# A recurrent layer's step: state's products copied and scanned in halves, two banks of negated sums put into PSUM by ScalarE

## The reference, cut to what matters

```python
def _L0_cond_ref(x, h0, Wx, Wh, b):          # x (16, 128, 128), h0 (16, 128)
    xw = jnp.einsum('ntd,dh->nth', x, Wx) + b
    def step(prev_h, xw_t):
        next_h = jnp.tanh(prev_h @ Wh + xw_t)
        return (next_h, next_h)
    _, hs = jax.lax.scan(step, h0, jnp.swapaxes(xw, 0, 1))
    return jnp.swapaxes(hs, 0, 1)
```

## Time and profile before

| | us |
|---|---|
| median of 3 runs | 8404.59 (8403.8 to 8407.73) |
| the profiled execution, whole | 8408.27 |
| its span, first to last instruction | 8406.4 |
| the recurrent loop's 127 intervals between new states | 320.5 to 5085.3 |
| a usual step | 37.12 |
| the step at a turn of the loop (7 of them) | 42.3 to 43.1 |

### The profile page before, as it was taken

How to read it: one execution, slowest core, us unless ns; L and a number is a source line. 1 busy time by engine, 2 the same in 40 slices (tenths; PEclk the granted TensorE clock), 3 DMA queues, 4 the chain that set the end, 5 groups by cost and what they waited for, 6 DMA issues and landing times. The chain is left out here.

```text
span 8406.4 us, 121771 instructions
## 1 busy us (share of the span) xinstructions
PE 7003.6 (83%) x39089; PEld 2814.9 (33%) x39089; DVE 7019.4 (84%) x12568; ACT 4731.0 (56%) x5718; POOL 1750.4 (21%) x1386
## 2 busy tenths in 40 slices
PE   4799999899998999999999994488888888782889
PEld 1333333333333333333333331122222222341453
DVE  4799999999999999999999996899999999446333
ACT  3677777777777777777777773233333333222322
POOL 0000001011010000101101000377777777000000
PEclk8999999999999999999999997799999999896999
DMA  1111111111111111111111111000000000000000
GB/s 38 35 27 31 29 29 32 27 31 27 32 31 27 31 30 29 32 26 32 28 30 32 26 32 29 18 4 3 4 3 4 3 4 3 2 6 3 3 15 5
DMA packets 51335, 174.64 MB, mean 21 GB/s; under 512 B 5857, under 2 KB 13794, under 8 KB 49698
## 3 DMA queue, kind: packets, MB, share of 16 engines
q0 software_dynamic: 37264, 145.91, 9.8%
q1 hardware_dynamic: 13586, 22.47, 1.0%
HBM read 15.12 MB, written 7.34 MB: 3 GB/s over the span
## 5 line engine op out<-in xcount | busy, mean ns | idle before, releaser
L944 POOL TENSOR_TENSOR hc<-hh,cg 128x512 f32<-128x512 f32 x1024 | 1294.8, 1267 | 512.1 <-DVE hh L927 512.1
L320 PE MATMUL r_ps<-wdiag,whq 128*128 128x512 bf16 x4864 | 1165.4, 382 | 233.1 <-ACT rx_d L389 174.4
L872 ACT ACTIVATE ps_m<-ps_m,aneg 128x508 f32<-128x508 f32 x1024 | 673.2, 658 | 1192.9 <-DVE hh L927 1071.5
L927 DVE TENSOR_TENSOR_SCAN hh<-ps_m,bx 128x512 f32<-128x512 f32 x1024 | 1257.2, 1235 | 0.0
L459 POOL TENSOR_TENSOR r_gate<-ident 128x1 f32<-128x1 f32 x137 | 213.7, 1560 | 4561.3 <-DVE rx_s L547 4496.2
L843 PE MATMUL ps_m<-hc,pick 128*128 128x512 f32 x2048 | 1053.4, 598 | 2.1 <-POOL hc L944 0.8
L554 DVE TENSOR_TENSOR_SCAN co<-rh_d 128x772 f32<-128x772 f32 x512 | 862.6, 1748 | 207.5 <-ACT rh_d L389 207.5
L554 DVE TENSOR_TENSOR_SCAN co<-rx_d 128x772 f32<-128x772 f32 x544 | 924.1, 1762 | 0.0
L909 DVE TENSOR_TENSOR bx<-ps_m,bg 128x512 f32<-128x512 f32 x1024 | 699.2, 689 | 49.3 <-PE ps_m L856 49.2
L320 PEld LDWEIGHTS r_ps<-wdiag,whq 128*128 128x128 bf16 x4864 | 417.8, 98 | 934.7 <-DVE rh_gain L183 219.8
L854 PE MATMUL ps_m<-rows,ones 128*128 128x512 bf16 x1024 | 405.3, 396 | 268.7 <-ACT ps_m L872 264.4
(11 more groups left out here) (407 smaller groups left out, 11796.8 us busy)
## 6 DMA issues: line engine op xcount, KB each, us to landing
rx_nd<-rx_s POOLq DMA_DIRECT2D x137, 1040.0 KB, 8.0
rows_scratch<-pc SPq DMA_DIRECT2D x48, 128.0 KB
rows<-rows_scratch SPq DMA_DIRECT2D x128, 48.0 KB
ew<-in_e SPq DMA_DIRECT2D x3, 1024.0 KB, 7.7
co<-in_x_dn SPq DMA_DIRECT2D x1, 1024.0 KB, 4.8
xcur<-in_x_dn SPq DMA_DIRECT2D x1, 1024.0 KB
out_x<-xcur SPq DMA_DIRECT2D x1, 1024.0 KB, 3.9
qi<-in_f_q SPq DMA_DIRECT2D x1, 384.0 KB, 3.0
```

Source lines behind the costliest of these rows:

```text
L320: e.matmul(ps[:, bank, :], whq[:, 0, :], wdiag[:, 0, 0:N, :].rearrange("p m k -> p (m k)"), start=True, stop=True)
L872: e.activation(da[un % NDA][:, :, 1:T], ps[:, un % 2, :].rearrange("p (n t) -> p n t", n=NG4)[:, :, 1:T], ACT.Exp, scale=aneg[:, 0:1]).the ...
L927: e.tensor_tensor_scan(hh[un % NBUF][:], da[un % NDA].rearrange("p n t -> p (n t)"), bx[un % NBUF][:], 0.0, ALU.mult, ALU.add).then_inc(sc ...
L944: e.tensor_tensor(hc[un % NHC][:], hh[un % NBUF][:], cg[:], ALU.mult).then_inc(weighted, 1)
```

## The change

The state's side of `rnn()` is changed in five places, and the X side in one.

- ACT copies R's products in two instructions in place of four, one for each half of the sequences (all four banks, 1024 elements). `rp_mm` is told once, after the last matmul of all banks.
- DVE's odd scan is split by halves of the sequences, for R and for X. R's two halves each wait for their copy. X's first half stays ahead of R's scans, X's second half comes after R's differences, ahead of X's even sums. `xs` counts three a step.
- PE forms negated sums by matmul for banks 4 and 5 alone. For banks 6 and 7 ACT writes the negated sums into PSUM, and PE waits for that ahead of the differences' matmul on bank 6.
- ACT's `put_sums` for R is split into odd and even places. ACT's order after the copies: odd sums, `Sign`, the write into PSUM, `Tanh`, even sums, differences.
- PE has 2 fillers in place of 5 between `residue` and R's remainder.

```diff
-        KA = NB + 4 + 2 * NRC + 1
-        VSUM = 3 + NRC + 1
+        A_COPIED, A_ODD, A_SEEDED, A_SIGNED, A_PUT = 2, 3, 5, 6, 8
+        KA = A_PUT + 2 * NRC + 1
+        V_ODD, V_EVEN, V_DIFF = 2, 3, 4
+        VSUM = V_DIFF + NRC + 1
...
+        OWN = NB // 2
+        HALVES = (slice(0, N // 2), slice(N // 2, N))
...
 # PE, h_product
                     for b in range(NB):
                         ins = e.matmul(ps[:, bank0 + b, :], h_stat(b, q), h_mov(b, r), start=(i == 0), stop=(i == 5))
-                        if i == 5:
-                            ins.then_inc(rp_mm, 1)
+                ins.then_inc(rp_mm, 1)
 # PE, remainder(..., own=NB, seeded=None)
                 e.wait_ge(*prefixed)
-                for b in range(NB):
+                for b in range(own):
                     e.matmul(ps[:, bank0 + b, :], negid[:], piece(F, "s", b), start=True, stop=False)
                 e.wait_ge(*differenced)
                 for b in range(NB):
+                    if b == own:
+                        e.wait_ge(*seeded)
+                    e.matmul(ps[:, bank0 + b, :], ident[:], diff(b), start=False, stop=False, skip_group_check=(b >= own))
-                    e.matmul(ps[:, bank0 + b, :], ident[:], diff(b), start=False, stop=False)
 # PE, a step
-                    residue(0, (ra, KA * t + NB)).then_inc(rl_mm, 1)
-                    stay_warm(4, 5)
-                    remainder(4, R, h_stat, h_mov, (v, KV * t + V0 + 2), (v, KV * t + V0 + 3), h_diff, False)
-                    sticky(4, (ra, KA * t + NB + 2))
+                    residue(0, (ra, KA * t + A_COPIED)).then_inc(rl_mm, 1)
+                    stay_warm(4, 2)
+                    remainder(4, R, h_stat, h_mov, (v, KV * t + V0 + V_EVEN), (v, KV * t + V0 + V_DIFF), h_diff, False,
+                              OWN, (ra, KA * t + A_SEEDED))
+                    sticky(4, (ra, KA * t + A_SIGNED))
 # ACT
+            def put_sums_of(F, c, done):
+                e.activation(F["at"][:, :, c, 2::3], F["s"][:, :, 2 + c:K2:2], ACT.Copy).then_inc(done, 1)
 # ACT, a step
-                    for b in range(NB):
-                        e.wait_ge(rp_mm, NB * t + b + 1)
-                        e.activation(R["pd"][:, :, 2 + KB * b:2 + KB * (b + 1)], ps[:, b, :].rearrange("p (n k) -> p n k", n=N),
-                                     ACT.Copy).then_inc(ra, 1)
+                    e.wait_ge(rp_mm, t + 1)
+                    for part in HALVES:
+                        e.activation(R["pd"][:, part, 2:K2].rearrange("p n (b k) -> p n b k", k=KB),
+                                     ps[:, 0:NB, :].rearrange("p b (n k) -> p n b k", n=N)[:, part], ACT.Copy).then_inc(ra, 1)
+                    e.wait_ge(v, KV * t + V0 + V_ODD)
+                    put_sums_of(R, 1, ra)
                     e.wait_ge(rl_mm, t + 1)
                     e.activation(R["sg"][:, 0], ps[:, 0:4, :], ACT.Sign).then_inc(ra, 1)
+                    e.wait_ge(v, KV * t + V0 + V_EVEN)
+                    e.wait_ge(xn, g + 1)
+                    e.activation(ps[:, 4 + OWN:4 + NB, :].rearrange("p b (n k) -> p n b k", n=N),
+                                 R["s"][:, :, 2 + KB * OWN:K2].rearrange("p n (b k) -> p n b k", k=KB), ACT.Copy,
+                                 scale=-1.0).then_inc(ra, 1)
                     e.activation(R["sg"][:, 1], ps[:, 0:4, :], ACT.Tanh, scale=1.0 / LEAST).then_inc(ra, 1)
-                    e.wait_ge(v, KV * t + V0 + 2)
-                    put_sums(R, ra)
-                    e.wait_ge(v, KV * t + V0 + 3)
+                    put_sums_of(R, 0, ra)
+                    e.wait_ge(v, KV * t + V0 + V_DIFF)
                     put_differences(R, R["gain"][:], ra)
 # DVE
-            def prefix_odd(F):
-                return e.tensor_tensor_scan(flat(F["s"][:])[:, 1::2], flat(F["pd"][:])[:, 0::2], flat(F["pd"][:])[:, 1::2],
-                                            0.0, ALU.add, ALU.add)
+            def prefix_odd(F, part):
+                return e.tensor_tensor_scan(flat(F["s"][:, part])[:, 1::2], flat(F["pd"][:, part])[:, 0::2],
+                                            flat(F["pd"][:, part])[:, 1::2], 0.0, ALU.add, ALU.add)
 # DVE, a step
-                    x_prefix_odd(g)
+                    x_prefix_odd(g, HALVES[0])
                     tl = Tally(e, v, KV * t + V0)
-                    e.wait_ge(ra, KA * t + NB)
-                    j = tl.inc(prefix_odd(R))
+                    for c in range(2):
+                        e.wait_ge(ra, KA * t + c + 1)
+                        j = tl.inc(prefix_odd(R, HALVES[c]))
                     tl.wait(j)
                     j = tl.inc(prefix_even(R))
                     tl.wait(j)
                     tl.inc(difference(R["gain"][:], R))
+                    x_prefix_odd(g, HALVES[1])
                     x_prefix_even(g)
                     x_chain(g - 1, s)
```

More of the change, by code:

```diff
@@ L287, in residue, with remainder @@
                 return ins
-            def remainder(bank0, F, stat, mov, prefixed, differenced, diff, last):
+            def remainder(bank0, F, stat, mov, prefixed, differenced, diff, last, own=NB, seeded=None):
                 e.wait_ge(*prefixed)
-                for b in range(NB):
+                for b in range(own):
                     e.matmul(ps[:, bank0 + b, :], negid[:], piece(F, "s", b), start=True, stop=False)
@@ L294, in remainder @@
                 for b in range(NB):
-                    e.matmul(ps[:, bank0 + b, :], ident[:], diff(b), start=False, stop=False)
+                    if b == own:
+                        e.wait_ge(*seeded)
+                    e.matmul(ps[:, bank0 + b, :], ident[:], diff(b), start=False, stop=False, skip_group_check=(b >= own))
                 for i, (q, r) in enumerate(LARGE_FIRST):
                     for b in range(NB):
-                        ins = e.matmul(ps[:, bank0 + b, :], stat(b, q), mov(b, r), start=False, stop=(last and i == 8))
+                        ins = e.matmul(ps[:, bank0 + b, :], stat(b, q), mov(b, r), start=False, stop=(last and i == 8),
+                                       skip_group_check=(b >= own))
                 return ins
@@ L304, in sticky @@
                     for c in range(2):
-                        ins = e.matmul(ps[:, bank0 + b, :], tau[:, c, :], R["sg"][:, c, b, :], start=False, stop=(c == 1))
+                        ins = e.matmul(ps[:, bank0 + b, :], tau[:, c, :], R["sg"][:, c, b, :], start=False, stop=(c == 1),
+                                       skip_group_check=(b >= OWN))
                 ins.then_inc(re_mm, 1)
@@ L336, in _ @@
                     e.wait_ge(stl, 2)
-                remainder(0, X, xl_stat, x_mov(g % UN), (xs, 2 * g + 2), (xd, 16 * (g + 1)), x_diff, True).then_inc(xl_mm, 1)
+                remainder(0, X, xl_stat, x_mov(g % UN), (xs, 3 * g + 3), (xd, 16 * (g + 1)), x_diff, True).then_inc(xl_mm, 1)
             e.wait_ge(xa, 5 * AHEAD + 1)
@@ L350, in _ @@
                     stay_warm(4, 5)
-                    residue(0, (ra, KA * t + NB)).then_inc(rl_mm, 1)
-                    stay_warm(4, 5)
-                    remainder(4, R, h_stat, h_mov, (v, KV * t + V0 + 2), (v, KV * t + V0 + 3), h_diff, False)
-                    sticky(4, (ra, KA * t + NB + 2))
+                    residue(0, (ra, KA * t + A_COPIED)).then_inc(rl_mm, 1)
[3 more added lines that the diff above has]
+                    sticky(4, (ra, KA * t + A_SIGNED))
                     if s == UN - 1:
                         e.wait_ge(stl, i + 3)
-                    remainder(0, X, xl_stat, x_mov((s + 1) % UN), (xs, 2 * g + 2), (xd, 16 * (g + 1)), x_diff, True).then_inc(xl_mm, 1)
+                    remainder(0, X, xl_stat, x_mov((s + 1) % UN), (xs, 3 * g + 3), (xd, 16 * (g + 1)), x_diff, True).then_inc(xl_mm, 1)
                     if s == UN - 2:
                         e.wait_ge(stp, i + 3)
-                    e.wait_ge(ra, KA * t + NB + 4 + 2 * NRC)
+                    e.wait_ge(ra, KA * t + A_PUT + 2 * NRC)
                     product(4, xp_stat, x_mov((s + 2) % UN)).then_inc(xp_mm, 1)
@@ L391, in parts @@
             def parts(g, bank0):
-                e.wait_ge(xs, 2 * g + 2)
+                e.wait_ge(xs, 3 * g + 3)
                 put_sums(X, xa)
@@ L554, in chain, with x_prefix_odd @@
                 return e.tensor_tensor_scan(co[:, at], F["d"][:, 0, 1:][:, at], F["d"][:, 1, 0:N * LX][:, at], 0.0, ALU.add, ALU.add)
-            def x_prefix_odd(g, later=True):
+            def x_prefix_odd(g, part, later=True):
                 e.wait_ge(xa, 5 * g + 1)
@@ L559, in x_prefix_odd @@
                     e.wait_ge(xd, 16 * g)
-                prefix_odd(X).then_inc(xs, 1)
+                prefix_odd(X, part).then_inc(xs, 1)
             def x_prefix_even(g):
-                e.wait_ge(xs, 2 * g + 1)
+                e.wait_ge(xs, 3 * g + 2)
                 prefix_even(X).then_inc(xs, 1)
@@ L574, in _ @@
             for g in range(AHEAD):
-                x_prefix_odd(g, g > 0)
```

(4 more changed lines are left out.)

## The result

| | before | after |
|---|---|---|
| median of the runs, us | 8404.19 (4 runs, 8401.8 to 8407.73) | 8308.14 (4 runs, 8295.8 to 8311.89) |
| profiled execution, us | 8408.27, span 8406.4 | 8311.89, span 8310.0 |
| mean granted clock of its span | 0.955 | 0.951 |
| recurrent loop, 127 steps, us | 4764.9 | 4672.7 |
| usual step, us | 37.12 | 35.87 |

The change is faster: ratio 0.9883, with an interval from 0.9869 to 0.9898. It gives 96 us where 132 were forecast. The loop gives 92 of them. The usual step came out within 0.05 us of the forecast; most of what is missing lies in the steps that are not usual.

A forecast was written before the change was run, and what follows sets the result against it. The state's chain ending at R's chain on DVE was taken as the bound, DVE's own work 1.67 us ahead. 1.22 less 0.17 gives 1.05 us a step, 134 us over 128 steps: 8272 us, range 8232 to 8347.

The forecast's parts named there:

- The wait ahead of R's chain: DVE waits there for ACT's remainder copies, 1.62 us a step; shortening the state's chain gains until DVE's own work ends last.
- the seed: ACT's write of negated sums for banks 6 and 7 into PSUM: 1.04 us, bounds 0.8 and 1.6, hidden even at 1.6.
- the prediction's other estimate: DVE's two added scans, by the Trainium skill's fixed latency of 58 cycles an instruction: 0.12 us.
- PE's gap ahead of X's identity matmuls: PE ends X's negated sums by 2144.2 and idles 1.3 us until X's DMA lands and the matmuls start at 2145.50.
- The three fillers taken out: Between `residue` and R's remainder on PE: removing them frees 0.65 us that would otherwise end at 2131.76, after the new start 2131.14.
- cover left: PE's slack from X's landing through fillers to the next products: 0.15 us plus 0.12; L201 safe by 1.2.
- The late landings: X's DMA landing late delays PE's chain: 1.75 us charged in 9 of 120 steps, 0.3 in some 16 others, 0.17 a step.
- the third rival: PE's clock falls at the new gap ahead of X's identity matmuls: 5.4 us in each such step, slower; chance 0.07.
- the sum: R's chain 1.29 us earlier, mean 1.22 after POOL's copies, less 0.17 for late landings: 1.05 a step, 134 us; chance 0.70.
- the first rival: X's part becomes the bound: gain 0.45 to 0.8 us a step, 8302 to 8347 us; chance 0.17.
- signs named for being wrong: L295 waiting for ACT, PEclk under 0.97 in the loop, or late-ending fillers with DVE idle over 0.5 us ahead of R's first scan.
- The second: The split of copies, scans or seed costs more than said: 8390 to 8420 us; chance 0.06.

The follow-up runs named there:

- the run with five: The changed kernel with 5 fillers in place of 2 after `residue`, ahead of the negated sums, as before the change: 8307.3 us, ratio 0.9875.
- kernel with fillers in the gap: The changed kernel with 5 more filler matmuls on PE, after `sticky` and ahead of X's negated sums: 8279.14 us, ratio 0.9848.
- X whole: The changed kernel with X's odd scan in one piece ahead of R's two halves, as before the change: 8220.96 us, ratio 0.9776.
- version with X in 12 and 4 and six fillers: The changed kernel with X's scan split 12 to 4 sequences, 6 fillers ahead of X's negated sums, 23 instead of 28 behind X's remainders: 8193.91 us, ratio 0.9748.
- kernel with the late DMA: The changed kernel with a second POOL gate instruction ahead of X's DMA in every step, without added fillers: 8475.4 us.

## Why the prediction was right, and where not

**The bound and the order.** Right. The wait ahead of R's chain was the step's, and when it was shortened, DVE's own work became the last, as the prediction said.

**The terms.** A copy of 1024 elements was put at 1.04 us and takes 1.02 (mean of 244), a half scan at 1.24 and takes 1.23, the seed at 1.04 (bounds 0.8 and 1.6) and takes 1.03. The Trainium skill, "ScalarE: Activation LUTs", section "What ACT_TABLE_LOAD costs", gives 186 ns plus 0.833 ns an element for an instruction with immediate scale and bias, an estimated 1.04 for 1024; the trace agrees, from PSUM and into it alike. The differences end at 9.50 after the state (10.47 before, 0.97 earlier; 0.94 said), PE's identity matmuls start at 9.55 (11.73), `sticky` ends at 17.14 (19.22), R's chain starts at 18.89 against a forecast of 18.86. DVE pays 0.30 (`xwt` ends at 18.77 in place of 18.47; 0.34 said), of it 0.07 the longer first wait, so the two added scans cost some 0.23, and the prediction's other estimate for them, 0.12, was too low. PE's gap ahead of X's identity matmuls was forecast at 1.3 us and is 0.95, since X's negated sums end at 20.6 and not at 20.3. The usual step: 35.87, forecast 1.29 under 37.12, which is 35.83.

**What hides, and what for.** The seed is hidden: done at 10.22, needed about 11.3. The three fillers taken out were worth nothing, as said; the run with five shows it. The forecast said that X's part of the step has cover left, and in usual steps it has: L203 never waits there.

**The late landings.** Their mechanism was right. Their price was too high, 1.75 us for a landing 2 us late against 1.1 measured for 1.75 us with the clock kept, and their number too low: landings 9.2 us or more behind the issue came 11 times in 127 steps before and 25 times after. By luck the two nearly cancel: 0.17 us a step was charged, and without the falls the late landings of the change cost some 0.19, against steps at the same places of the body that have none.

**The step that failed** is the third rival, PE's clock. It was given 0.07 and a price of 5.4 us in each step that it strikes, and the argument against it was that no gap becomes longer than the 1.88 us that the usual step has at full clock. That argument took the forecast gap, 1.3, and left out the late landings, which the same text counted two parts earlier: 1.3 + 1.2 is 2.5, well over 1.88. The two stood in the text as separate cases, one in the sum and one as a rival, where they are one: the lateness makes the gap. So the rival came true in part, in 17 of 120 steps. Its size was off too: 5.4 us were forecast, and a fall costs 1.6 here, since only the eight identity matmuls run slowly (5.40 for 3.70) and the exact products behind them do not. 17 falls at 1.6 are some 27 of the missing 36 us. The rest lies in small terms: with all landings in time the steps but the turns would gain some 1.15 us on the mean where 1.22 was summed, and the seven turns gave 0.70 each in place of 1.05. The kernel with fillers in the gap, which has no such fall, gains 1.03 us a step on the mean of the steps but the turns (36.18 against 37.22), where 1.05 was the sum, and its median is 7 us from the forecast of 8272; that it comes so near owes something to its 13 late landings in place of 25.

The measured time lies inside the range that was given, but that is luck in part: the upper end was drawn from the first rival, X's part as the bound, and not from the falls that used it up. Two of the signs named for being wrong did come: PEclk is 0.96 between 200 and 5500 us, where 0.97 was the limit, and behind the latest landings DVE idles up to 1.4 us ahead of R's first scan, where 0.5 was.

That PE's clock falls where it waits for a DMA between groups of matmuls shows in the rows of this case: at clock 0.67 on average the eight matmuls of 2250.81 take 5.40. The Trainium skill describes such a loop in "TensorE: Matmul & The Clock Gate", section "HAM oscillation — how this bites in real kernels". The trace agrees that it is the wait for the DMA that does it; the waits in that section's loop are some 3 to 5 us long, and here 2.2 to 2.4 were enough in 17 steps. What the runs don't give is a length from which it happens: with a gap of 2.63 and of 2.66 us in two steps in a row the one kept the clock and the other did not, and in the change itself 2.25 and 2.27 came out differently.

**The other rivals.** The result, 8308, lies among the times of the first (X's part as the bound, 8302 to 8347), but not by its mechanism: the usual landing moved from 21.2 to 21.5 after the state, which is the 0.33 of the sum, and usual steps kept their gain. The second (the split not doing what it says) is ruled out by the durations above. Nor is the kernel slower.

**By parts of the change.** Not asked in the prediction, and the larger lesson: the split of X's scan costs more than it gives. The prediction saw its price, 0.34 us on DVE, and set it against the earlier start of R's scans as one sum. Taken apart, X whole has R's chain 0.25 earlier, closes the gap on PE and is 87 us faster; the seed and R's halves carry the gain. With X's first part at 12 of 16 sequences R's scan starts 0.05 later than with halves, and R's chain 0.51 earlier than with halves.

**Left open.** Why landings are late in certain steps of the loop, and why more or fewer of them in one kernel than another (25 in the change, 3 in the version with X in 12 and 4 and six fillers), was not settled. In the change the late landings and the falls come at places 4, 5, 11 and 12 of 16, the steps counted from 0 behind each turn, which points to something that repeats with the code. Nor was it settled why the clock falls behind some late landings and not behind others.

## What to carry to other kernels

A shortened engine that stands ahead of a DMA gets an idle gap: add the latest landing, not the median one, to it before saying that the clock will hold, and put a few idle matmuls into the gap rather than ahead of other waits. Costs that meet in the same step (a gap and a late landing) belong in one case, not in two that exclude each other. Split an instruction only as far as its first part fills the wait behind which it stands; equal halves left DVE waiting 0.41 us and put a whole half on the path.

## What the hardware did that was not expected

In the traces a DMA of POOL (1040 KB from SBUF to SBUF) lands 8.0 us after its issue in most steps and up to 10.1 in others, and the late ones have a packet of an instruction queue (q8) beside them. The change, DMA in two stretches of 11 us, the first with a late landing (queue, kind: packets, MB, share; then the issue with its us to landing):

```profile
q0 software_dynamic: 272, 1.07, 54.9%
q8 instruction: 1, 0.02, 0.5%
...
rx_nd<-rx_s POOLq DMA_DIRECT2D x1, 1040.0 KB, 9.3
```

```profile
q0 software_dynamic: 272, 1.07, 54.5%
...
rx_nd<-rx_s POOLq DMA_DIRECT2D x1, 1040.0 KB, 8.0
```

One packet of 0.02 MB goes with 1.3 us. In the loop of the change all 31 landings over 8.3 us have such a packet and none of the 95 at 8.0 to 8.1; before, all 39 and none of 88. In the version with X in 12 and 4 and six fillers it is all 45 and one of 80, and in the kernel with fillers in the gap all 17 and 11 of 105. But in the kernel with the late DMA such a packet runs beside 25 landings of 8.0 to 8.1 us, and none there is over 8.3. So the packet alone isn't enough; it is a correlation read from the traces, and no run moved a packet on purpose.

The granted clock fell behind gaps from 1.86 us on in some steps, and stayed behind gaps of up to 2.8 us in most steps of the kernel with the late DMA. In the change, five idle matmuls ahead of the wait, 1.08 us of work, took all 17 falls away, with 13 late landings left to cause one.
